# Heads stage: queries and keys of a batch projected into one bank, values into another, and two gathers moved ahead of the splits

## The reference, cut to what matters

```
qkv = (x @ w_qkv.T).reshape(B, N, 3, H, D).transpose(2, 0, 3, 1, 4)
q, k, v = (qkv[0], qkv[1], qkv[2])
k = jnp.concatenate([extra_k, k], axis=2)     # from the context, per batch
v = jnp.concatenate([extra_v, v], axis=2)
attn = jax.nn.softmax(jnp.einsum('bhnd,bhmd->bhnm', q * scale, k), axis=-1)
out = jnp.einsum('bhnm,bhmd->bhnd', attn, v)
return out @ w_proj.T + b_proj                # then x = x + tanh(g_xattn[1]) * this
```

## Time and profile before

| | |
|---|---|
| median of 3 executions | 1029.14 us |
| profiled execution | 1029.96 us, of it 1028.2 us from first to last instruction |
| mean granted TensorE clock | 0.884 of full speed |
| busy, share of the span | PE 79%, PEld 53%, DVE 63%, ACT 37%, POOL 36% |
| heads stage | about 202 to 474 us of the span |
| chain that ended last, by engine | PE 56%, DVE 23%, issue 7%, POOL 7%, ACT 4%, DMA 2% |

### The profile page before, as it was taken

How to read it: one execution, slowest core, us unless ns; L and a number is a source line. 1 busy time by engine, 2 the same in 40 slices (tenths; PEclk the granted TensorE clock), 3 DMA queues, 4 the chain that set the end, 5 groups by cost and what they waited for, 6 DMA issues and landing times.

```text
span 1028.2 us, 14705 instructions
## 1 busy us (share of the span) xinstructions
PE 809.4 (79%) x5027; PEld 548.4 (53%) x5027; DVE 652.1 (63%) x1844; ACT 377.8 (37%) x759; POOL 366.6 (36%) x502
## 2 busy tenths in 40 slices
PE   3636999547788789887989899988989879994374
PEld 1625888324444344434349666667634556773363
DVE  4674222376777777754886759997367448986321
ACT  2123444125654566662350554442300124441210
POOL 5225333484455542203854201101201004554254
PEclk9857999768998999998999899996799889996597
DMA  8606777100000000000000000000000050002220
GB/s 212 228 0 181 217 207 199 32 16 8 12 12 9 10 2 2 1 2 1 0 1 1 1 1 1 1 1 1 1 1 0 1 164 1 1 1 82 70 61 26
DMA packets 51772, 45.46 MB, mean 44 GB/s; under 512 B 6804, under 2 KB 47655, under 8 KB 51442
## 3 DMA queue, kind: packets, MB, share of 16 engines
q1 hardware_dynamic: 48146, 36.91, 12.2%
q0 software_dynamic: 3552, 7.61, 2.8%
HBM read 36.90 MB, written 7.80 MB: 43 GB/s over the span
## 4 chain that ended last, share of the span: by engine, by line
PE 56%; DVE 23%; issue 7%; POOL 7%; ACT 4%; DMA 2%; POOLq 0%; SPq 0%; DVEq 0%; ACTq 0%
PE psum L2458 6%; PE psum L1131 4%; PE psum L2053 3%; PE psum L1420 3%; PE psum L2732 3%; PE psum L2762 2%; DVE stats L154 2%; PE psum L1334 2%; PE psum L1397 2%; DVE XN L168 2%; DVE scratch L1655 2%; PE psum L610 2%; PE psum L1114 2%; PE psum L277 2%; PE psum L1142 2%
## 5 line engine op out<-in xcount | busy, mean ns | idle before, releaser
L1655 DVE TENSOR_REDUCE scratch<-psum 128x2 f32<-128x512 f32 (+1 forms) x160 | 106.7, 685 | 56.6 <-PE psum L1377 30.7
L1575 ACT ACTIVATE scratch<-psum 128x512 f32<-128x512 f32 x160 | 94.2, 604 | 94.5 <-PE psum L1397 94.5
L233 POOL TENSOR_SCALAR veps<-moments 128x4 f32<-128x4 f32 (+1 forms) x48 | 10.5, 219 | 299.7 <-DVE moments L157 298.4
L277 PE MATMUL psum<-ident,XN 128*128 128x128 f32 x144 | 31.5, 359 | 43.9 <-DVE XN L168 40.0
L903 DVE SCALAR_TENSOR_TENSOR scratch<-psum,b_block_bias,scratch 128x256 f32<-128x256 f32 (+1 forms) x48 | 18.6, 430 | 72.0 <-ACT scratch L1056 67.9
L975 POOL DMA_INDIRECT scratch<-pair_rows,b_gather_at x39 | 39.2, 1005 | 68.8 <-PE psum L1104 43.9
L2458 PE MATMUL psum<-late,scratch 128*128 128x512 f32 x128 | 57.0, 606 | 5.7 <-DVE routing_wide L2401 5.0
L2664 POOL TENSOR_TENSOR scratch<-scratch,arena 128x1024 f32<-128x1024 f32 x16 | 30.4, 1901 | 76.9 <-DVE arena L2882 76.9
L1397 PE MATMUL psum<-scratch,arena 128*128 128x256 bf16 x256 | 51.3, 283 | 6.0 <-ACT scratch L1561 4.4
L292 ACT ACTIVATE XT<-psum 128x512 f32<-128x512 f32 (+1 forms) x40 | 22.2, 559 | 83.4 <-PE psum L277 83.3
L1377 PE MATMUL psum<-arena 128*128 128x512 bf16 x128 | 52.0, 412 | 0.5 <-DVE scratch L1655 0.4
(11 more groups left out here) (452 smaller groups left out, 2075.2 us busy)
## 6 DMA issues: line engine op xcount, KB each, us to landing
arena<-in_L_ffn_w SPq DMA_DIRECT2D x72, 128.0 KB, 2.9
arena<-in_L_ffn_wg SPq DMA_DIRECT2D x24, 256.0 KB, 3.2
wide<-in_L_xattn_Wkv SPq DMA_DIRECT2D x1, 2048.0 KB
wide<-in_L_ffn_W SPq DMA_DIRECT2D x1, 2048.0 KB, 8.7
late<-in_L_ffn_W SPq DMA_DIRECT2D x8, 256.0 KB, 7.0
pair_results<-scratch SPq DMA_DIRECT2D x15, 128.0 KB, 3.6
X<-in_x SPq DMA_DIRECT2D x2, 512.0 KB, 4.8
C<-in_ctx SPq DMA_DIRECT2D x2, 512.0 KB, 6.8
```

The costliest lines, as they stand in the source:

```text
L277: last = t.transpose(c.bank[self.banks[g % 2]][:, i * P:(i + 1) * P], self.src[:, j, :], c.ident[:])
L1575: a.activation(out, bank[3 + e % 2][:, :], ACT.Exp).then_inc(s["exp"], 1)
L1655: v.tensor_reduce(out, bank[m % 3][:, :].rearrange("p (h t) -> p h t", t=n), AX.X, ALU.max, negate=True).then_inc(s["maxed"], 1)
```

## The change

Tile 0 and tile 1 of a batch now share bank 7: four blocks of 128 columns, queries and keys of tile 0, then of tile 1, all projected in step 1. The values of both tiles go to bank 6 in step 3. ScalarE copies queries of both tiles in one instruction of 256 columns, keys in a second, in step 2, and values in a third in step 4, now ahead of `copy_again`. The semaphore `split` counts three a batch in place of six, and each waiter names the copy it needs. GpSimd issues both gathers before `queries`. In VectorE's step 10 `evacuate(b - 1, 0)` goes ahead of `split_maxima(b, 0, 0)`.

```diff
@@ pool @@
         def queries(b):
-            g.wait_ge(s["split"], 6 * b + 6)
+            g.wait_ge(s["split"], 3 * b + 1)
...
         def keys(b):
-            g.wait_ge(s["split"], 6 * b + 6)
+            g.wait_ge(s["split"], 3 * b + 2)
...
             if half < 2 * NG:
-                gather(g, half, 0, 1)
+                gather(g, half, 0, 2)
             queries(b)
-            if half < 2 * NG:
-                gather(g, half, 1, 1)
             keys(b)
@@ pe @@
-        def project(b, i, k):
+        def project(b, k):
             self.norm.turn.wait_halves(t, b + 1)
-            j = 2 * b + i
-            t.matmul(bank[k][:, 0:3 * D], c.XT[:, j * P:(j + 1) * P], self.Wqkv[:],
-                     start=True, stop=True).then_inc(s["qkv"], 1)
+            for i in range(2):
+                j = 2 * b + i
+                last = t.matmul(bank[k][:, 2 * D * i:2 * D * i + 2 * D], c.XT[:, j * P:(j + 1) * P],
+                                self.Wqkv[:, 0:2 * D], start=True, stop=True)
+            last.then_inc(s["qkv"], 1)
+
+        def project_values(b, k):
+            for i in range(2):
+                j = 2 * b + i
+                last = t.matmul(bank[k][:, D * i:D * i + D], c.XT[:, j * P:(j + 1) * P],
+                                self.Wqkv[:, 2 * D:3 * D], start=True, stop=True)
+            last.then_inc(s["qkv"], 1)
...
-                    project(b + 1, 0, 7)
+                    project(b + 1, 7)
             if at == 3:
...
-                    project(b + 1, 1, 6)
+                    project_values(b + 1, 6)
                 if behind:
                     if ahead:
-                        t.wait_ge(s["split"], 6 * (b + 1) + 3)
+                        t.wait_ge(s["split"], 3 * (b + 1) + 2)
                     turn_again(b - 1, 1, 7)
             if at == 5 and late:
                 if ahead:
-                    t.wait_ge(s["split"], 6 * (b + 1) + 6)
+                    t.wait_ge(s["split"], 3 * (b + 1) + 3)
                 turn_out(b - 2)
...
             if at == 8 and ahead:
-                t.wait_ge(s["split"], 6 * (b + 1) + 6)
+                t.wait_ge(s["split"], 3 * (b + 1) + 2)
...
             if at == 13 and b < B:
+                if ahead:
+                    t.wait_ge(s["split"], 3 * (b + 1) + 3)
@@ act @@
-        def split(b, i, k):
-            a.wait_ge(s["qkv"], 2 * b + i + 1)
-            if b >= 3 and i == 0:
-                a.wait_ge(s["av"], 4 * (b - 2))
-            if b and i == 0:
-                a.wait_ge(s["k_rows"], b)
-            rows = [bank[k][:, n * D:(n + 1) * D].rearrange("p (h c) -> p h c", c=8) for n in range(3)]
-            a.activation(self.rest[:, 0, 16 * i:16 * i + 16, :], rows[0], ACT.Copy, scale=self.SCALE) \
-                .then_inc(s["split"], 1)
-            a.activation(self.rest[:, 1, 16 * i:16 * i + 16, :], rows[1], ACT.Copy).then_inc(s["split"], 1)
-            a.activation(self.v_rows(b % 3, i)[:, :, 0:8], rows[2], ACT.Copy).then_inc(s["split"], 1)
+        def split(b, k):
+            a.wait_ge(s["qkv"], 2 * b + 1)
+            if b:
+                a.wait_ge(s["k_rows"], b)
+            rows = bank[k][:, :].rearrange("p (i n h c) -> p n i h c", i=2, n=2, c=8)
+            for n in range(2):
+                a.activation(self.rest[:, n].rearrange("p (i h) c -> p i h c", i=2), rows[:, n], ACT.Copy,
+                             scale=1.0 if n else self.SCALE).then_inc(s["split"], 1)
+
+        def split_values(b, k):
+            a.wait_ge(s["qkv"], 2 * b + 2)
+            if b >= 3:
+                a.wait_ge(s["av"], 4 * (b - 2))
+            a.activation(self.V[:, b % 3, :, 0:144].rearrange("p i (h c) -> p i h c", c=9)[:, :, :, 0:8],
+                         bank[k][:, 0:2 * D].rearrange("p (i h c) -> p i h c", i=2, c=8), ACT.Copy) \
                 .then_inc(s["split"], 1)
...
             if at == 2 and ahead:
-                split(b + 1, 0, 7)
+                split(b + 1, 7)
             if at == 4:
+                if ahead:
+                    split_values(b + 1, 6)
                 if behind:
                     copy_again(b - 1, 1, 7)
-                if ahead:
-                    split(b + 1, 1, 6)
@@ dve @@
             if at == 10:
+                if behind:
+                    evacuate(b - 1, 0)
                 if b < B:
                     split_maxima(b, 0, 0)
-                if behind:
-                    evacuate(b - 1, 0)
...
-        v.wait_ge(s["split"], 6)
+        v.wait_ge(s["split"], 1)
```

## The result

The changed kernel took **1003.04 us** in the median of four runs (1002.98 to 1003.57), against 1030.24 (1024.53 to 1032.05) for the kernel before: a ratio of 0.9746, with a 95% interval of 0.9707 to 0.9786. It is faster, as forecast, but by 27 us and not by 13.5, and lies under the range's low end of 1009.

The account below looks back on a forecast made before the run. The heads stage was taken as a loop of waits with no engine full. Gains of 7.5, 4.2, 1.7 and 0.6 us made 14.0, less 0.3 and 0.2: 13.5 us off 1029.96, so 1016.5 us; range 1009 to 1024.

Parts of the forecast that it names:

- the small corrections: Taken off the 14.0 us: 0.3 us for the projection in the whole stage and 0.2 us for iteration 0.
- the term of the sum: Iterations 2 to 4 of the heads stage: 2.5 us gained in each, 7.5 us together.
- 1.39 us swap: VectorE step 10: the evacuation, no longer behind split_maxima, comes 1.39 us earlier.
- the first rival: TensorE's clock stays high as well: 3 to 6 us more gained, about 1012 us; chance 0.13.
- My objection: Against the clock rival: iteration 5, with the shorter wait, also came to the lower level a little later.
- Contention: VectorE's add_results beside GpSimd's work: two of four additions slowed, +0.86 us, part of it absorbed.
- slower rival: VectorE's two-input instructions each sit out a GpSimd cast: 3.6 us per iteration, 1033 us; chance 0.05.
- VectorE takes it back: Rival: add_results loses 1.7 us, split_maxima stays at 1.39; about 7 us gained, 1023 us; chance 0.24.
- the change does little: Rival: TensorE's waits turn into waits for scores or masks; 4 us gained in all, 1026 us; chance 0.08.
- the bounds listed for the range: Five iterations (-2.5, +1.5), starts and projection (-0.6, +2.4), 2 us of scatter: 1012 to 1021 us.
- Iteration 0: Queries one gather, 1.3 us, later and keys some 0.4 us earlier: booked +0.2 us, between -0.4 and +1.3.
- 2 us of scatter: Allowance in the forecast's own bounds for differences between executions of the kernel.

Follow-up runs that it names:

- warm: The kernel before, with three extra fp32 products on TensorE in the wait ahead of turn_parts of iterations 1 to 6; 1016.38 us, ratio 0.9889.
- noswap: The changed kernel with split_maxima ahead of the evacuation in step 10, as before; 1018.68 us, ratio 0.9892.
- swap: The kernel before, with only the evacuation moved ahead of split_maxima in step 10; 1022.35 us, ratio 0.9943.
- add3: The changed kernel with VectorE's result additions in step 3 in place of 5; 1010.02 us, ratio 0.9808.
- The repeated kernel: The changed kernel run again without any edit, against the kernel before; 1003.35 us, ratio 0.9747.

## Why the direction was right and the size wrong

**The waits: right.** Booked 14.0 us before the small corrections, 13.5 in all; measured 14.3 between two kernels, warm and the changed one, with the same clock. From `turn_parts` of step 11 in one iteration to that of the next it is 29.9 us in warm and 27.4 after: 2.5 us, the term of the sum. `turn_parts` waits 1.63 us (said: 1.0 to 1.8), GpSimd 3.90 (about 4, ended by `turn_again`), the split takes 0.67 (near 0.7). Counted from the `turn_parts` ahead of it, that of step 11 starts 285.84 - 271.14 = 14.70 us later, against 16.88 before (from 274.56): 2.2 us earlier, said 2.35. That it got there by a 1.39 us swap was half wrong: 0.7 us of it is GpSimd moving away, and with the level held the swap is worth 4.4 of the 14.3 us. That the total agrees to 0.3 us is partly luck: the swap was priced too high, and the early queries and keys too low, at 6 to 7 us by themselves (what I expected of noswap) where 9.9 were measured.

**TensorE's clock: the step that failed.** The prediction put it: "I book nothing: up to 1.5 us in each of 2 to 4 iterations, 3 to 6 us, is the first rival". Warm shows a term of 8.15 us in the stage, 1.0 to 2.5 us in each of five iterations. Two things were wrong. I called it a rival, though the rows argued for it: 0.94 and 0.89 in the earlier trace rows, and nothing that would keep it once the wait shrank. And I sized it from two iterations; the lower level came in all of iterations 2 to 6, from 290.9, 321.6, 355.7, 386.4 and 417.1 us, 20.5 us together. Each of the five begins within 1.2 us of the start of the `turn_parts` that had waited 2.19 to 2.75 us, the first two while it still waited. With waits of 1.63 no such stretch came in any profile of the changed kernel's stage. The length of that wait alone doesn't decide it, though: iteration 1 waited 2.66 us and kept the level, noswap lost it in iterations 1, 3 and 5 and kept it in 2 and 4 with nearly equal waits, and swap lost it with waits of 1.35 and 1.47 us close together. What decides was not found. My objection, that iteration 5 "came to the lower level a little later", was evidence for the rival: that `turn_parts` too had waited, 2.19 us.

**Contention: mis-sized, and partly hidden.** Booked +0.86 for two of four additions; all four were hit, 2.57 - 1.41 = 1.16 us, and add3 shows that the additions without it, two steps earlier, return 1.5 us over the whole stage. The slower rival's price of 3.6 us per iteration is not borne out: it needed additions of over 4.5 us, they take 2.57, the fourth lost only 0.08 us, and the split none. The Trainium skill (SBUF — State Buffer, "Who interferes with whom") has such a pair exclude each other for whole instructions. By that rule all four would be blocked; the trace agrees that all four take longer, by 0.08 to 0.49 us, and no run here shows how an addition and a GpSimd instruction are interleaved.

**VectorE takes it back, and the change does little: fell.** The one allowed about 1.1 us per iteration, the other less than 1; with the clock's part taken out the iterations are 2.5 us shorter. The sums of the former and of the slower rival also count six iterations with a gather, where the forecast books five, 1 to 5; and the bounds listed for the range add up to 1011.4 and 1022.4, not 1012 and 1021. Neither changes the account.

**Iteration 0: near enough.** Booked 0.2 us worse; counted from the projection of batch 0 it takes 41.72 us against 41.96, with 22.8 us at the lower level against 26.3, so what the order did and what the clock did are not separated. TensorE's waits only changed places:

```profile
229.39 1.01 PE L1342 MATMUL psum<-ident,scratch 128*128 128x128 bf16 x8 [7.47 <-POOL scratch L1277]
...
233.22 1.01 PE L1342 MATMUL psum<-ident,scratch 128*128 128x128 bf16 x8 [1.54 <-POOL scratch L1285]
```

7.47 us for the queries in place of 4.71, and 1.54 for the keys in place of 3.29.

**Behind the stage: open.** 4.0 us of the profiled difference lie in code that is the same. The repeated kernel shows that one program gives 554.9 in one execution and 562.1 in another, so no part of it can be called the change's work. Whether the change raises the odds of the shorter one, which would explain that its first four runs lay within 0.6 us, was not settled. The range allowed 2 us of scatter; one program gave 9.7. The sum with the clock in it, 1016.5 - 8.2 = 1008.3, is already under the range's low end; less the 4.0, it is 1004.3. The other 1.3 us to the profiled 1002.98 are 0.8 of waits and 0.5 ahead of the stage.

## What to carry to other kernels

Where the granted clock of a loop is below 1.00, find every stretch at the lower level and the waits around its start, and book their time with the wait that you remove, as a term of the sum. Two iterations are too few to size it. To separate the two, put useless products into the wait of the old kernel, and compare iterations that already had the upper level: what is gained beyond them is the clock's part. And price contention at the place to which an engine moves as well as at the one that it leaves.

## What the runs showed of the hardware

- A kernel got faster by doing more: 2.1 us of needless products in each wait took 8.15 us off the stage, since 20.5 us at 1.2 GHz disappeared. In noswap 10.2 us of it were worth 4.96, and two iterations of one execution with nearly equal waits differ by 1.6 us, one with 3.4 us at the lower level and one with none.
- With the upper level held, the stage repeats to 0.2 us: 201.74, 201.72, 201.91 and 201.68 in four executions. What scatters by 7 us is the part behind it, where lower stretches are many (120 and 147 us at 1.2 GHz in two executions of one program): 7.2 us for 27.1 more, 0.27 each, less than the 0.40 and 0.48 of the loop.
- Nearly the same wait cost the level in some iterations and not in others: of six waits of 2.01 to 2.42 us ahead of noswap's `turn_parts`, three did.
- VectorE's two-input additions took 0.34 and 0.35 us alone, and 0.65, 0.64, 0.83 and 0.43 beside GpSimd's casts and subtractions; its maxima from the banks stayed at 0.68 and 0.69 us throughout.
